# Cross-attention and FP4 feed-forward on one core: batches written out, 128-row context tiles, and jobs placed in a step by the engine that takes them

## The chip, the core and the metric

The kernel runs on one core of a Trainium2 chip. The core has a matrix engine (TensorE, PE in the rows), a vector engine (VectorE, DVE), an activation engine (ScalarE, ACT), GpSimd (POOL) and a queue engine (SyncE, SP) that issues most DMAs. Each engine takes its own instructions in program order and waits for the others by semaphores. The metric is the device time of one execution in microseconds, the median of several; lower is better.

## What is computed

Eight batches. Each has 512 query rows and 1601 context rows of 256 numbers. A layer norm, 16-head cross-attention with a residual, a second layer norm, and a gated feed-forward whose inputs and weights are rounded to a 4-bit grid in blocks of 16:

```python
x = x + xattn(layernorm(x), ctx, ctx)          # heads of 16, softmax over the 1601 keys, biases
def fp4_linear(x, w):                          # blocks of 16 along the last dim
    return einsum('bsk,nk->bsn', fp4_quant_dequant(x), fp4_quant_dequant(w))
h = silu(fp4_linear(y, w_gate)) * fp4_linear(y, w_up)      # y = layernorm(x), 256 -> 704
x = x + fp4_linear(h, w_down)                              # 704 -> 256
```

## The kernel before

**Steps.** The heads are taken in four groups of four, the context in 13 tiles, so a batch has 52 steps (`STEPS`). In step n, PE writes the scores of the tile for two heads (`scores(n, 0)`, L612), then those of the other two (`scores(n, 1)`), into the same two PSUM banks `st`; ACT takes each with an exponential into `prob` (L763, `exps`). Then PE makes products of queries and keys again for the row maxima of a later group (`pair_products`, L626, into `mx`), which DVE reduces (L811, or L820 and L822 for single pieces), and then multiplies the exponentials of step n-1 with the values (`weighted`, L641, into `pvb`).

**Jobs.** Everything else is cut into jobs and hung into the steps by the table `SLOTS`. An entry has two lists. A job of the first list, called side 0 here, is done by PE between `scores(n, 0)` and `scores(n, 1)`; ACT takes its result between its two pairs of exponentials, DVE before the reduction of the step. A job of the second list (side 1) is done by PE behind `weighted`, taken by ACT behind its second pair of exponentials and by DVE behind the reduction. The jobs: `ctxT`, `xnT`, `attT`, `xqT`, `hqT` (transposes, copied by ACT), `q` (L528, ACT L704 and L705), `k` (L538, ACT L715 and L716), `v` (L545, ACT L721), `nm` (transpose of the maxima, L549, five DVE operations from L845), `pvT` (L553, DVE L855 and L857), `o`, `gate`, `up` (L575), `down` (L585), and in the first batch `wT` (transposed FP4 weights, L592, ACT L747). In the loop they all write one PSUM bank, `misc`, in turn: a job's first matmul waits until the job before it has been taken out.

**Batches.** Parts of three batches overlap: "early" jobs prepare the next batch, "att" jobs belong to the present one, "late" jobs end the previous one. The program is a prologue `pre`, the batch `first`, a hardware loop (`Fori`) over six batches, the batch `last`, and `tail`, the feed-forward of the last batch. In the prologue, the first 36 pieces of maxima are made. Inside the loop, waits compare with values held in registers.

**Other queues.** `DVE_EXTRA` places layer norm and quantisation on DVE (among them `xlast`, L926, and `hscale`), `POOL_WORK` the splitting of q and k into bf16 parts and the rounding (L1048 and L1050, L1054 to L1062). SP issues the DMAs in a fixed order; k and q go to scratch memory and come back as `kstack` and `qstack`. The context comes in as `cin` by two DMAs, of 124 and of 123 rows per tile; the raw feed-forward weights (`raw_in`) stand in SP's queue between the others.

Of the kernel before, what the change touches and what calls it, by code (L numbers as in the profile page):

```python
# [16 lines left out]
KROWS = [124, 124] + [123] * 11  # L17
# [36 lines left out]
M_LEAD = 18  # L54
BIAS_AT = STEPS - M_LEAD - 1

# [5 lines left out]

SLOTS = {
    0: ([("v", 5, "att")], []),
    1: ([("v", 6, "att")], [("pvT", 3, "late")]),
    2: ([("attT", 0, "late")], [("attT", 1, "late")]),
    3: ([("o", 0, "late")], []),
    4: ([("o", 1, "late")], []),
    5: ([("ctxT", 0, "early")], []),
    6: ([("ctxT", 1, "early")], [("ctxT", 2, "early")]),  # L70
    7: ([("ctxT", 3, "early")], [("ctxT", 4, "early")]),
    8: ([("ctxT", 5, "early")], [("nm", 1, "att")]),
    9: ([("ctxT", 6, "early")], [("xnT", 0, "early")]),
    10: ([("xnT", 1, "early")], []),
    11: ([("q", 0, "early")], [("wT", 0, "once")]),
    12: ([("k", 0, "early")], [("wT", 1, "once")]),
    13: ([("k", 1, "early")], [("wT", 2, "once")]),
    14: ([("k", 2, "early")], [("pvT", 0, "att")]),
    15: ([("k", 3, "early")], [("wT", 3, "once")]),
    17: ([("q", 1, "early")], []),  # L80
    18: ([("xqT", 0, "late")], [("xqT", 1, "late")]),
    19: ([("gate", 0, "late")], []),
    20: ([("gate", 1, "late")], [("wT", 4, "once")]),
    21: ([("k", 4, "early")], [("nm", 2, "att")]),
    22: ([("gate", 2, "late")], [("wT", 5, "once")]),
    23: ([("gate", 3, "late")], []),
    24: ([("k", 5, "early")], [("wT", 6, "once")]),
    25: ([("gate", 4, "late")], [("wT", 7, "once")]),
    26: ([("gate", 5, "late")], []),
    27: ([("k", 6, "early")], [("pvT", 1, "att")]),  # L90
    28: ([("gate", 6, "late")], []),
    29: ([("gate", 7, "late")], []),
    30: ([("k", 7, "early")], [("wT", 8, "once")]),
    31: ([("up", 0, "late")], [("wT", 9, "once")]),
    32: ([("up", 1, "late")], []),
    33: ([("up", 2, "late")], []),
    34: ([("up", 3, "late")], [("nm", 3, "att")]),
    35: ([("up", 4, "late")], [("wT", 10, "once")]),
    36: ([("up", 5, "late")], [("wT", 11, "once")]),
    37: ([("up", 6, "late")], []),  # L100
    38: ([("up", 7, "late")], []),
    39: ([("hqT", 0, "late")], [("hqT", 1, "late")]),
    40: ([("down", 0, "late")], [("pvT", 2, "att")]),
    41: ([("hqT", 2, "late")], []),
    42: ([("v", 0, "early")], [("hqT", 3, "late")]),
    43: ([("down", 1, "late")], []),
    44: ([("v", 1, "early")], [("hqT", 4, "late")]),
    45: ([("hqT", 5, "late")], []),
    46: ([("v", 2, "early")], []),
    47: ([("down", 2, "late")], [("nm", 0, "early")]),  # L110
    48: ([("v", 3, "early")], [("hqT", 6, "late")]),
    49: ([("hqT", 7, "late")], []),
    50: ([("down", 3, "late")], []),
    51: ([("v", 4, "early")], []),
# [3 lines left out]
    1: ([], [("pvT", 3, "late")]), 2: ([("attT", 0, "late")], [("attT", 1, "late")]), 3: ([("o", 0, "late"), ("o", 1, "late")], []),  # L118
# [12 lines left out]
def slots(kind, n):  # L131
    return (TAIL_SLOTS if kind == "tail" else SLOTS).get(n, ([], []))


PER = {}
for _step in SLOTS.values():
# [18 lines left out]
W_SCALE_AT = {1: 0, 4: 1, 14: 2, 17: 3, 25: 4, 29: 5}
W_POWER_AT = {3: 0, 6: 1, 16: 2, 19: 3, 27: 4, 31: 5}
POOL_WORK = {
    1: [("late", "bias", 0)], 11: [("early", "q", 0)], 12: [("early", "k", 0)], 13: [("early", "k", 1)],
    14: [("early", "k", 2), ("late", "xround", 0)], 15: [("early", "k", 3)], 17: [("early", "q", 1)],
# [7 lines left out]
class Iteration:  # L167
# [8 lines left out]
    def count(self, part, per, k):  # L176

        n = (self.ahead + SHIFT[part]) * per + k
        if isinstance(self.i, int):
            return self.i * per + n  # L180
        assert n > 0
        return self.i * per + n


class SharedBanks:
# [931 lines left out]
```

## Time and profile before

| | us |
|---|---|
| median of 3 runs | 2022.91 (2022.39 to 2029.71) |
| the profiled execution | 2027.88 |
| its span, first to last instruction | 2026.0 |
| prologue, to the first exponential | 127.9 |
| batch `first` | 246.4 |
| six loop batches | 1373.6 (225.4 to 230.5 each) |
| batch `last` | 200.9 |
| `tail` | 77.3 |

The stages are measured between the first exponentials (L763) of the batches. A step's length below is the time from the first exponential of one step to that of the next. In the rows of a timeline, the number in brackets is how long the engine had been idle before the instruction, with what ended the idle time.

### The profile page before, as it was taken

Reading aid. Unit: us, or ns where it says so; the run is one execution under the profiler, and the core shown is the slowest. Engines: PE = TensorE matmul, PEld = TensorE weight load, DVE = VectorE, ACT = ScalarE, POOL = GpSimd, SP = SyncE. Lnnn points to the kernel's source line nnn. Section 1 sums busy time; section 2 is a strip of 40 time slices with the busy share of each in tenths; the row PEclk is TensorE's granted clock in tenths of the full one; section 3 lists DMA queues with packets and bytes.
Section 4 is the critical chain, followed back from the end, with each engine's and each line's share of the span. In section 5 each row is a group of like instructions: output and inputs, shape, how many; then the busy total and the mean of one; then the engine's idle time right before and its main releaser. Section 6 shows DMA issues by size and latency. Waiting matters only on the chain. (4 is left out here: it accounts for less than half of the span.)

```text
span 2026.0 us, 30105 instructions
## 1 busy us (share of the span) xinstructions
PE 1754.9 (87%) x9600; PEld 730.4 (36%) x9600; DVE 1348.5 (67%) x1636; ACT 1127.0 (56%) x2239; POOL 541.8 (27%) x415
## 2 busy tenths in 40 slices
PE   3567688989999899899999899899999899989957
PEld 2222222333343334433343334433344334423425
DVE  1557576776857777676857777576867677576524
ACT  1124466666546665566546665566556665556631
POOL 3203550041320414042320514032320514000414
PEclk9677899999999999999999999999999999999988
DMA  2721431143212332134212322134212422020000
GB/s 66 154 65 27 92 72 33 54 92 65 42 39 52 78 58 40 59 74 79 46 35 52 82 58 38 61 73 71 54 32 49 89 58 39 17 33 1 6 16 11
DMA packets 97768, 109.53 MB, mean 54 GB/s; under 512 B 18484, under 2 KB 83004, under 8 KB 97596
## 3 DMA queue, kind: packets, MB, share of 16 engines
q1 hardware_dynamic: 95500, 106.21, 25.4%
q8 instruction: 89, 1.46, 0.3%
q10 hardware_dynamic: 2096, 1.18, 0.2%
q14 instruction: 83, 0.68, 0.1%
HBM read 76.78 MB, written 30.16 MB: 53 GB/s over the span
## 5 line engine op out<-in xcount | busy, mean ns | idle before, releaser
L763 ACT ACTIVATE prob<-st 123x512 f32<-123x512 f32 (+1 forms) x1664 | 906.9, 601 | 469.1 <-PE st L612 466.9
L811 DVE TENSOR_REDUCE cmx<-mx 128x4 f32<-128x2048 f32 x336 | 769.8, 2291 | 317.6 <-PE mx L626 315.9
L612 PE MATMUL st<-qstack,kstack 112*123 112x512 bf16 (+1 forms) x1664 | 554.6, 401 | 56.3 <-ACT prob L763 29.8
L641 PE MATMUL pvb<-prob,vv 123*17 123x512 f32 (+1 forms) x3328 | 446.2, 609 | 0.0
L612 PEld LDWEIGHTS st<-qstack,kstack 112*123 112x123 bf16 (+1 forms) x1664 | 201.4, 136 | 455.9 <-ACT prob L763 234.6
L626 PE MATMUL mx<-kstack,qstack 48*128 48x512 bf16 (+1 forms) x2048 | 256.6, 343 | 59.7 <-DVE cmx L811 38.1
L575 PE MATMUL misc<-wguT,rowsT 128*128 128x352 f32 x460 | 159.7, 469 | 19.1 <-DVE nmf L845 13.7
L820 DVE TENSOR_REDUCE cmx<-mx 128x2 f32<-128x1024 f32 x96 | 114.9, 1220 | 38.3 <-PE mx L626 38.2
L1021 POOL TENSOR_TENSOR cin<-cin 128x400 f32<-128x400 f32 (+1 forms) x60 | 60.8, 1013 | 284.3 <-ACT cin L716 284.2
L626 PEld LDWEIGHTS mx<-kstack,qstack 48*128 48x128 bf16 x2048 | 57.8, 95 | 216.9 <-issue 133.8
L1021 POOL TENSOR_TENSOR qx<-qx,qp 128x512 f32<-128x512 f32 x16 | 18.5, 1158 | 387.0 <-ACT qp L705 387.0
L641 PEld LDWEIGHTS pvb<-prob,vv 123*17 123x17 f32 (+1 forms) x3328 | 55.4, 95 | 159.8 <-issue 156.7
L538 PE MATMUL misc<-ctxT,wk 128*128 128x400 f32 (+1 forms) x236 | 93.2, 517 | 22.5 <-DVE att L857 12.4
L545 PE MATMUL misc<-wv,ctxT 128*123 128x256 f32 (+1 forms) x392 | 104.8, 413 | 7.1 <-DVE nmf L845 7.1
L575 PEld LDWEIGHTS misc<-wguT,rowsT 128*128 128x128 f32 x460 | 84.9, 191 | 65.8 <-DVE nmf L845 19.1
L1058 POOL TENSOR_TENSOR ht<-ht,mt 128x704 f32<-128x704 f32 x32 | 53.7, 1679 | 184.5 <-DVE mt L939 184.5
L585 PE MATMUL misc<-wdT,hqT 128*128 128x256 f32 x348 | 86.6, 390 | 4.7 <-ACT hqT L742 4.7
L1054 POOL TENSOR_TENSOR ht<-ht,rh 128x704 f32<-128x704 f32 x32 | 44.4, 1386 | 166.7 <-DVE rh L932 165.2
L545 PEld LDWEIGHTS misc<-wv,ctxT 128*123 128x123 f32 (+1 forms) x392 | 78.6, 202 | 27.3 <-DVE nmf L845 10.3
L1034 POOL TENSOR_TENSOR x<-x,bob 128x1024 f32<-128x1024 f32 x8 | 18.7, 2343 | 241.6 <-DMA x<-x 241.6
L867 DVE SCALAR_TENSOR_TENSOR ht<-hqT,misc 128x352 f32<-128x352 f32 x57 | 29.7, 521 | 75.8 <-ACT hqT L730 75.8
L585 PEld LDWEIGHTS misc<-wdT,hqT 128*128 128x128 f32 x348 | 62.4, 189 | 28.0 <-issue 10.7
(169 smaller groups left out, 1546.8 us busy)
## 6 DMA issues: line engine op xcount, KB each, us to landing
kstack<-scr_k SPq DMA_DIRECT2D x384, 100.1 KB, 4.4
scr_k<-cin SPq DMA_DIRECT2D x48, 300.0 KB, 4.3
qstack<-scr_q SPq DMA_DIRECT2D x384, 32.0 KB, 1.9
cin<-ctx_in SPq DMA_DIRECT2D x8, 1353.0 KB
scr_q<-qp SPq DMA_DIRECT2D x16, 384.0 KB, 4.2
scr_k<-cin SPq DMA_DIRECT2D x16, 300.8 KB, 4.5
xn<-x SPq DMA_DIRECT2D x8, 512.0 KB, 6.5
x<-x SPq DMA_DIRECT2D x8, 512.0 KB, 3.6
```

The costliest lines, as they stand in the source:

```text
L538: last = mm(o[:, 0:w], wk[:, h, m * 128:(m + 1) * 128], ctxT[:, h, COFF[n]:COFF[n] + w], start=(h == 0), stop=(h == NC2 - 1))
L545: last = mm(o[0:w, (kt % 2) * E:(kt % 2 + 1) * E], ctxT[:, h, KOFF[kt]:KOFF[kt] + w], wv[:, h, :], start=(kt % 2 == 0 and h == 0), stop=(h ...
L575: last = mm(o[:, 0:IH], rowsT[:, h, t * 128:(t + 1) * 128], wguT[:, h, first:first + IH], start=(h == 0), stop=(h == NC2 - 1))
L585: last = mm(o[:, 0:E], hqT[0:FW[f], f, :], wdT[0:FW[f], f, :], start=(f == 0), stop=(f == NF - 1))
L612: mm(st[0:KROWS[kt], h, :], kstack[:, hd, KOFF[kt]:KOFF[kt] + KROWS[kt]], qstack[:, hd, :], start=True, stop=True).then_inc(st_full, 1)
L626: last = mm(mx[:, q % 2, par, at:at + w], qstack[r0:r0 + LEAD, hd, t * 128:(t + 1) * 128], kstack[r0:r0 + LEAD, hd, k0:k0 + w], start=True ...
L641: last = mm(pvb[32 * h:32 * h + D + 1, :], vv[0:w, kt, HG * g + h, :], prob[0:w, n % 2, h, :], start=(kt == 0), stop=(kt == NKT - 1))
L763: activate(prob[0:KROWS[kt], n % 2, 2 * pair + h, :], st[0:KROWS[kt], h, :], ACT.Exp, scale=SCALE).then_inc(exp_done[2 * pair + h], 1)
L811: v.tensor_reduce(cmx[:, g % 2, h0:h0 + 2, at0:at1 + 1:at1 - at0], mx[:, :, :, :].rearrange("p j h n -> p h j n"), op=ALU.max, axis=AX.X). ...
L820: v.tensor_reduce(cmx[:, g % 2, h0:h0 + 2, at:at + 1], products, op=ALU.max, axis=AX.X).then_inc(max_free, 1)
L1021: g_.tensor_tensor(whole, whole, parts[:, 0, :], ALU.subtract).then_inc(step, 1)
L1058: g_.tensor_tensor(y, y, m, ALU.add).then_inc(h_step, 1)
```

## The change

- `Fori` becomes a Python loop: all eight batches are written out, and no wait compares with a register.
- Context tiles have 128 rows, the thirteenth 65 (before: 124, 124 and eleven of 123). The count of tiles, steps and matmuls stays. The context comes in by three DMAs: 128 rows by 2 tiles, 128 rows by 10, 65 rows.
- `SLOTS` is rewritten. Jobs taken by DVE (`nm`, `pvT`, with `gate`, `up`, `o`, `down` as before) are on side 0; jobs taken by ACT (`q`, all eight `k`, all seven `v`, most transposes) move to side 1. Many late jobs stand one step earlier.
- Prologue (`PRE_SLOTS`): x is loaded before the context; four `k` jobs stand before `xnT` and `q`; only the 26 pieces of the first group's maxima are made, and in the first five steps of `first` four pieces a step instead of two. Five `v` jobs stand at steps 34 to 42.
- Weights: `wk`, `wq` and their biases get a semaphore of their own; `wv`, `wo`, `bv`, `bo` are issued later, and the raw feed-forward weights go from SP's queue to ACT's.
- `tail`: the rounding of xa goes from POOL to DVE, and of the four row tiles of h, POOL and DVE round two each (`hround`).

```diff
-KROWS = [124, 124] + [123] * 11
+KROWS = [128] * (T // 128) + [T % 128]
...
-    12: ([("k", 0, "early")], [("wT", 1, "once")]),
...
+    11: ([("wT", 1, "once")], [("k", 1, "early")]),
...
+PRE_SLOTS = {
+    5: ([("ctxT", j, "early") for j in range(7)], []),
+    11: ([("k", j, "early") for j in range(4)], []),
+    14: ([("xnT", j, "early") for j in range(2)], [("q", 0, "early"), ("q", 1, "early")]),
...
-            with eng.Fori(0, B - 2) as i:
+            for i in range(B - 2):
                 body(Iteration("loop", i, 1))
...
-            for q in (first, first + 1):
+            for q in range(first, first + number):
...
-                sp.dma_start(ctx_rows[0:KROWS[2], 2:NKT, :], ctx_in[bi, n0:T, :].rearrange("(t p) n -> p t n", t=NKT - 2)).then_inc(s_ctx[1], 16)
...
+                for piece, (t0, t1) in enumerate(((0, 2), (2, NKT - 1))):
+                    sp.dma_start(ctx_rows[:, t0:t1, :], ctx_in[bi, t0 * 128:t1 * 128, :].rearrange("(t p) n -> p t n", p=128)).then_inc(s_ctx[piece], 16)
+                sp.dma_start(ctx_rows[0:KROWS[-1], NKT - 1, :], ctx_in[bi, n1:T, :]).then_inc(s_ctx[2], 16)
...
+                    elif what == "xround":
+                        dve.wait_ge(xm_ready, c(1, 1))
+                        v.tensor_tensor(xa[:, :], xa[:, :], mt[:, :], ALU.add).then_inc(xr_step, 1)
```

PE, in a loop batch where the first `k` jobs stand. Before:

```order
L641 MATMUL pvb<-prob,vv 17x512 x4
L612 MATMUL st<-qstack,kstack 123x512 x2
L538 MATMUL misc<-ctxT,wk 128x401 x2
L292 REGISTER_ALU
L612 MATMUL st<-qstack,kstack 123x512 x2
L292 REGISTER_ALU
L626 MATMUL mx<-kstack,qstack 128x512 x2
```

After:

```order
L630 MATMUL pvb<-prob,vv 17x512 x4
L524 MATMUL misc<-ctxT,wk 128x401 x2
L601 MATMUL st<-qstack,kstack 128x512 x4
L615 MATMUL mx<-kstack,qstack 128x512 x4
L630 MATMUL pvb<-prob,vv 17x512 x4
L524 MATMUL misc<-ctxT,wk 128x400 x2
```

The `k` job has moved from between the two pairs of scores to behind `weighted`; the four score matmuls now stand together.

PE, in a loop batch at the `nm` job of the third group. Before:

```order
L641 MATMUL pvb<-prob,vv 17x512 x4
L490 REGISTER_ALU
L548 REGISTER_ALU
L549 MATMUL misc<-ident,nmx 16x128
L612 MATMUL st<-qstack,kstack 123x512 x2
L575 MATMUL misc<-wguT,rowsT 128x352 x2
```

After:

```order
L601 MATMUL st<-qstack,kstack 128x512 x2
L536 MATMUL misc<-ident,nmx 16x128
L601 MATMUL st<-qstack,kstack 128x512 x2
L615 MATMUL mx<-kstack,qstack 128x512 x4
L630 MATMUL pvb<-prob,vv 17x512 x4
L524 MATMUL misc<-ctxT,wk 128x401 x2
L601 MATMUL st<-qstack,kstack 128x512 x2
L562 MATMUL misc<-wguT,rowsT 128x352 x2
```

The `nm` job has moved between the pairs of scores, and a `k` job stands between it and the next `gate` job.

SP, at the start of the prologue. Before:

```order
L351 DMA cin<-ctx_in 124x2x256
L352 DMA cin<-ctx_in 123x11x256
L345 DMA xn<-x 128x4x256
L372 DMA scr_q<-qp 128x1536
```

After:

```order
L357 DMA xn<-x 128x4x256
L364 DMA cin<-ctx_in 128x2x256
L364 DMA cin<-ctx_in 128x10x256
L365 DMA cin<-ctx_in 65x256
L376 DMA scr_q<-qp 128x1536
```

x now comes first, and the long context transfer has 128 rows.

## Rows read from the trace of the kernel before

**Rows 1.** A batch: start:end, length, PE, PEld, DVE, ACT, POOL busy, clock, DMA.

```profile
604.40:834.50 230.10, 212.28 (x1196) 89.26 (x1195) 163.50 (x196) 139.55 (x279) 61.83 (x49) 0.99 0.28 58
```

**Rows 2.** Timeline of a loop step without a job: start, length, engine, line, tiles.

```profile
675.21 2.20 ACT L763 ACTIVATE prob<-st 123x512 f32<-123x512 f32 x4 [0.18 <-PE st L612]
678.23 0.65 PE L612 MATMUL st<-qstack,kstack 112*123 112x512 bf16 x2
678.69 0.60 ACT L763 ACTIVATE prob<-st 123x512 f32<-123x512 f32 x1 [1.28 <-PE st L612]
```

**Rows 3.** Timelines of PE and of ACT at k jobs on side 0.

```profile
656.48 1.51 PE L538 MATMUL misc<-ctxT,wk 128*128 128x401 f32 x4
658.03 0.59 ACT L715 ACTIVATE cin<-misc,bqk 128x401 f32<-128x401 f32 x1 [0.75 <-PE misc L538]
659.00 1.08 ACT L763 ACTIVATE prob<-st 123x512 f32<-123x512 f32 x2
660.34 1.09 ACT L763 ACTIVATE prob<-st 124x512 f32<-124x512 f32 x2 [0.26 <-PE st L612]
664.41 1.09 ACT L763 ACTIVATE prob<-st 124x512 f32<-124x512 f32 x2
```

**Rows 4.** The same at a q job and at a v job on side 0.

```profile
651.92 1.88 PE L528 MATMUL misc<-xnT,wq 128*128 128x512 f32 x4
653.92 0.69 ACT L704 ACTIVATE qx<-misc,bqk 128x512 f32<-128x512 f32 x1 [0.93 <-PE misc L528]
655.07 2.20 ACT L763 ACTIVATE prob<-st 123x512 f32<-123x512 f32 x4
...
801.49 1.89 PE L545 MATMUL misc<-wv,ctxT 128*123 128x256 f32 x8
803.41 0.65 ACT L721 COPY vv<-misc 123x256 f32<-123x256 f32 x2 [0.86 <-PE misc L545]
```

**Rows 5.** A weight transpose on side 1, in the batch `first`.

```profile
199.75 0.52 PE L592 MATMUL misc<-ident,ht 88*128 88x88 f32 x4
200.31 0.45 ACT L747 COPY wguT<-misc 128x352 f32<-128x352 f32 x1 [0.17 <-PE misc L592]
200.66 1.09 ACT L763 ACTIVATE prob<-st 123x512 f32<-123x512 f32 x2
```

**Rows 6.** PE across an edge of the hardware loop.

```profile
834.01 0.64 PE L612 MATMUL st<-qstack,kstack 112*124 112x512 bf16 x2 [3.79 <-issue]
834.48 3.32 PE L545 MATMUL misc<-wv,ctxT 128*123 128x256 f32 x8
```

**Rows 7.** Waits of PE in the six loop batches: total us, times, longest.

```profile
PE misc L575 <- DVE nmf L845: 12.7, 12, 1.2
...
PE misc L575 <- DVE att L857: 2.3, 6, 0.4
```

**Rows 8.** Waits of the whole span in which a DMA was waited for.

```profile
DVE ah L957 <- DMA ht<-w_up: 13.8, 2, 11.5
...
DVE ah L957 <- DMA ht<-w_gate: 13.4, 1, 13.4
```

**Rows 9.** The prologue: a window with the DMA share, then timelines.

```profile
13.00:24.00 11.00, 0.00 (x0) 0.00 (x0) 0.00 (x0) 0.00 (x0) 3.33 (x3) 1.00 0.20 67
...
32.52 1.90 PE L517 MATMUL st<-ident,cin 123*128 123x123 f32 x8 [22.56 <-DMA cin<-ctx_in]
...
51.11 0.36 SPq L372 DMA_DIRECT2D scr_q<-qp  x1
...
76.89 1.03 PE L626 MATMUL mx<-kstack,qstack 48*128 48x512 bf16 x4 [5.72 <-DMA kstack<-scr_k]
...
127.86 1.08 ACT L763 ACTIVATE prob<-st 124x512 f32<-124x512 f32 x2 [0.94 <-PE st L612]
```

**Rows 10.** The tail, POOL: two starts of its quantising, one row tile apart.

```profile
1995.78 1.39 POOL L1054 TENSOR_TENSOR ht<-ht,rh 128x704 f32<-128x704 f32 x1
...
2003.21 1.39 POOL L1054 TENSOR_TENSOR ht<-ht,rh 128x704 f32<-128x704 f32 x1
```

More of the change, by code:

```diff
@@ L84 @@
[L84 to L105, printed above, removed]
@@ L106 @@
-    43: ([("down", 1, "late")], []),
[L107 to L114, printed above, removed]
+    4: ([("o", 1, "late")], [("ctxT", 0, "early")]),
+    5: ([("ctxT", 1, "early")], [("ctxT", 2, "early")]),
+    6: ([("ctxT", 3, "early")], [("ctxT", 4, "early")]),
@@ new lines @@
+    7: ([("ctxT", 5, "early")], [("ctxT", 6, "early")]),
+    8: ([("nm", 1, "att")], [("xnT", 0, "early")]),
+    9: ([("xnT", 1, "early")], [("q", 0, "early")]),
+    10: ([("wT", 0, "once")], [("k", 0, "early")]),
+    11: ([("wT", 1, "once")], [("k", 1, "early")]),
+    12: ([("wT", 2, "once")], [("k", 2, "early")]),
+    13: ([("wT", 3, "once")], [("k", 3, "early")]),
+    14: ([("pvT", 0, "att")], []),
+    15: ([], [("q", 1, "early")]),
+    17: ([("xqT", 0, "late")], [("xqT", 1, "late")]),
@@ new lines @@
+    18: ([("gate", 0, "late")], []),
+    19: ([("gate", 1, "late"), ("wT", 4, "once")], []),
+    20: ([("gate", 2, "late"), ("wT", 5, "once")], []),
+    21: ([("nm", 2, "att")], [("k", 4, "early")]),
+    22: ([("gate", 3, "late")], []),
+    23: ([("gate", 4, "late"), ("wT", 6, "once")], []),
+    24: ([("wT", 7, "once")], [("k", 5, "early")]),
+    25: ([("gate", 5, "late")], []),
+    26: ([("gate", 6, "late")], []),
+    27: ([("pvT", 1, "att")], [("k", 6, "early")]),
+    28: ([("gate", 7, "late")], []),
@@ new lines @@
+    40: ([("pvT", 2, "att")], [("hqT", 2, "late")]),
+    41: ([("hqT", 3, "late")], []),
+    42: ([], [("v", 0, "early")]),
+    43: ([("down", 1, "late")], []),
+    44: ([], [("v", 1, "early")]),
+    45: ([("hqT", 4, "late")], [("hqT", 5, "late")]),
+    46: ([("down", 2, "late")], []),
+    47: ([("nm", 0, "early")], [("v", 2, "early")]),
+    48: ([("hqT", 6, "late")], [("hqT", 7, "late")]),
+    49: ([("down", 3, "late")], []),
+    50: ([], [("v", 3, "early")]),
+    51: ([], [("v", 4, "early")]),
+}
@@ L176, in count @@
     def count(self, part, per, k):
[L178 to L182, printed above, removed]
+        return self.batch(part) * per + k
 class SharedBanks:
@@ L374, in keys_out @@
             def keys_out(it, m):
-                if it.kind == "loop":
-                    sp.lower_val(it.count("early", 4, 1))
                 for g in (2 * m, 2 * m + 1):
@@ L653, in body @@
                         scores(n, 1)
-                    for job in maxima(it, n):
+                    products = maxima(it, n)
+                    for job in products[:2]:
                         pair_products(job)
@@ L659, in body @@
                         weighted(STEPS - 1, "late")
+                    for job in products[2:]:
+                        pair_products(job)
                     for job in jobs(it, n, 1):
@@ L996, in body @@
                             extra(part, what, k)
-                assert all(made[p] == LINKS[p] for p in ("early", "late") if p in it.parts), made
+                assert it.kind == "tail" or all(made[p] == LINKS[p] for p in ("early", "late") if p in it.parts), made
             iterations(dve, body)
```

215 lines of the change are left out of this document (115 added, 100 removed).

## The prediction

> **What bounds the kernel now.** I read the batches first, then one bare step, then the waits. A loop batch takes 230.1 us, and PE is busy in 212.28 of them at a clock of 0.99, full speed; DVE has 163.5, ACT 139.6, POOL 61.8 [rows 1]. So the loop is PE's, with some 18 us of holes, and two questions decide: which holes go, and which are made. In a bare step the exponentials start at 675.21 and the next step's at 678.69, 3.48 us later, while the next scores start at 678.23, 3.02 us after the first exponential [rows 2]. These 3.02 us are a chain of PE and ACT: both exponentials of the first pair, the scores of the second pair, maxima products, `weighted`. ACT is idle for 1.28 us at its end [rows 2]. So PE has a short hole between its two pairs of scores, where it waits for the first exponentials, and none behind `weighted`. A job on side 0 falls into this hole; a job on side 1 lengthens the chain by all of its own time, and its ACT part comes ahead of the next exponential.
>
> **Side 1 for the jobs of ACT.** The length of a step with such a job is 3.02, plus the time from the job's first matmul to ACT's first operation on it, plus ACT's part until the next exponential. A job that stands on side 1 now tests this: weight transpose 199.75, ACT's copy 200.31, exponential 200.66, which is 0.56 + 0.35 behind the point where `weighted` leaves PE [rows 5]; the next exponential indeed starts with the end of the copy, not with its scores.
> - k: 658.03 - 656.48 = 1.55 and 659.00 - 658.03 = 0.97, so 3.02 + 1.55 + 0.97 = 5.54. On side 0 a k step takes 664.41 - 660.34 = 4.07 [rows 3]; with the other k steps I take 4.0. Eight jobs: +12.3 us per batch.
> - q: 2.00 and 1.15 [rows 4], so 6.17, against some 4.3 on side 0 (a matmul pair longer than k's by 0.37 us, rows 3 and 4). Two jobs: +3.8.
> - v: 1.92 and some 0.55 of its two copies [rows 4], so 5.5, against 4.3 on side 0. Six jobs and a half one: +7.8.
> - Transposes on side 1: three more than now, but fewer next to a v job: +1.
> Against it: a side 0 job that follows such a step is covered, since PE writes the next scores early and runs the job while ACT is still at the k result. Four gate or up jobs behind k, and three down jobs behind v, gain 0.2 to 0.3 each: -1.5.
>
> **Side 0 for the jobs of DVE.** `nm` and `pvT` on side 1 are taken only behind the reduction, and the next job, also for `misc`, waits for that. Seven rows of PE's waits name DVE's first operation on `nm` or the last on `pvT`; they go from 12.7 to 2.3 and sum to 44 us in six batches, 7.4 per batch [rows 7]. The steps are longer by somewhat more, 8.3. On side 0 they wait for no reduction of their own step; `nm` may wait a little for the one before (0.2 us each): -8.3 + 0.8. The own PE time of these eight jobs falls into the hole: -2.
>
> **The loop's edge.** At an edge PE is idle for 3.79 us with nothing that it waits for, and the v job behind it takes 3.32 us instead of the 1.89 of its like [rows 6, 4]: 5.2 us per edge, five edges. Written out they go: -5.2 each, which I count per batch. The Trainium skill, Runtime: NRT & Kernel Launch, section Instruction fetch mechanics, says that instructions are fetched ahead in sequence only and that a taken branch to a page not held breaks this; the idle time at the edge agrees, and nothing in the straight-line batches speaks against it. Without the registers a wait with two semaphores costs ACT some 0.06 us more in a bare step (3.54 in the straight-line batches against 3.48 in the loop, an estimate from step lengths): +0.6.
>
> Sum of a loop batch: 12.3 + 3.8 + 7.8 + 1 - 1.5 - 8.3 + 0.8 - 2 - 5.2 + 0.6 = +9.3 us. Six batches: **+56**. Batch `last` has few of the moved jobs (one and a half v) and loses some of the stalls: 0.
>
> **Prologue, now 127.9 us.** Context rows are waited for until 32.5, and from 13 to 24 us the DMA engines are 0.20 busy at 67 GB/s, as if three of sixteen ran [rows 9]. The Trainium skill, DMA: Bandwidth & Descriptors, section Why a DMA increments its semaphore by 16 and not by 1, says that a transfer is cut over the largest number up to 16 that divides its slowest dimension: 3 for 123 rows, 16 for 128. The row agrees with the 3. The sum goes by the row: 67 GB/s at a share of 0.20 are 335 GB/s at a full one, so x, context and two weights (2.7 MB) need 8 us at best and 16 at half the share; with 2 us to start I take 13 for the landing. From there: transposes and four k pieces (ACT first issues six weight DMAs, some 4 us), then xnT, q and POOL's split, which end 23 us later, at some 36. From the end of this split to the first maxima product the queue SP needs what it needs now, 76.89 - 51.11 = 25.8 [rows 9]: 62. The rest, 127.86 - 76.89 = 51.0 now, loses ten of 36 pieces (1.15 us each) and one v job, but the way of the maxima through DVE and SP (5.5 us), now hidden behind those ten pieces, is exposed: 45. First exponential at 106 to 107: **-21.5** (-12 to -30).
>
> **Batch `first`, now 246.4.** Raw weights are waited for by DVE for 13.4 and 11.5 us [rows 8], because SP's queue holds them behind the slow context; both go with the earlier issue, and with them some 9 us of a late context: about -34. The ten pieces come back: in five steps two reductions of 2.3 us and their products stand in a row, some 3 us each more than now, +12. The moved jobs cost what they do in the loop, without the late ones: +16. Sum **-6** (-22 to +8).
>
> **Tail, now 77.3.** The quantising of a row tile of h follows at 7.43 us (2003.21 - 1995.78) [rows 10], four in series between DVE and POOL. With two engines DVE becomes the one that sets the end; I take one round as saved, **-8** with the rounding of xa (-12 to -2).
>
> Total: -21.5 - 6 + 56 + 0 - 8 = +20.5 on the profiled execution's 2027.9. That execution lies 5 us above the median, 2022.9, and the loop's edges, the part that varies, are gone afterwards, so I do not carry the 5 us in full: **2044 us**, 1.0% above the median.
>
> **Rivals.**
> 1. Faster: the moved ACT jobs cost half of what the chain says, since the following step makes the time up (PE has written its scores by then, and any side 0 job is covered). The 24 us per batch become 12, in seven batches -84: **1960**, or 1975 with a smaller gain elsewhere. For it: the covered jobs above. Against it: the four k steps stand in a row with nothing on side 0 between them, and in a row nothing can be made up. The point from which it decides: at a cost of 1.2 instead of 1.4 us per moved job the kernel comes out level.
> 2. No difference (2013 to 2033): the same mechanisms, with the two sums closer, 7 us per batch instead of 9.3.
> 3. Slower than forecast, **2075**: DVE becomes a bound as well. In `first` it holds ten more pieces and the weights' scales, and `hscale` (2.4 us) meets a reduction (2.29) and an `up` in steps of 3.7: 2 us per batch more, and a colder PE clock in the holes.
> 4. The prologue gains nothing, because the weights and the queue of small transfers set it, not the context: +15, 2059.
>
> **How the numbers follow.** About 0.5% is what a measurement of this kernel can tell from no change: 2012.8 to 2033. The forecast has 0.5, the first rival 0.17, the second 0.18, the third 0.1, the fourth 0.05. With a spread of some 20 us around the forecast that makes faster 0.2, same 0.22, slower 0.58. The range, 2000 to 2072, leaves out most of the first rival and the far end of the third.
>
> **What would show it.** Right: a k job's row on PE behind `weighted`, ACT idle up to it, the next exponential at its end, steps of 5.5 us four times in a row; PE's waits on DVE's `nm` and `pvT` operations gone; no PE idle time of 3.8 us between batches; loop batches of 238 us that are all alike; first exponential near 106; a context transfer at a DMA share far above 0.2. Wrong: loop batches at 225 or less, which is the first rival; PE waiting at L615 for DVE's reduction, the third; first exponential behind 115, the fourth.

## The result, and the profile after

The changed kernel takes **2104.98 us** (median of 4 runs, 2101.66 to 2106.55) against 2023.93 us for the kernel before on the same chip: a ratio of 1.0393, 95% interval 1.0367 to 1.0418. It is slower, as forecast, but by four times as much (+81 us, not +20), and it lies above the range. Its profiled execution took 2106.43 us, with a span of 2104.6.

The stages of the two spans, cut at the first exponential of each batch (the tail begins at the end of the last exponential), beside the forecast's own terms:

| stage (us) | before | forecast | after | missed by |
|---|---|---|---|---|
| prologue, to the first exponential | 127.9 | 106.4 | 103.0 | -3.4 |
| batch `first` | 246.4 | 240.4 | 254.5 | +14.1 |
| six loop batches | 1373.6 | 1429.4 | 1473.2 | +43.8 |
| batch `last` | 200.9 | 200.9 | 197.5 | -3.4 |
| tail | 77.3 | 69.3 | 76.4 | +7.1 |

So the miss lies in the loop batches, in `first` and in the tail. The same cut of a loop batch as in [rows 1] reads, for the kernel after (start:end, length, PE, PEld, DVE, ACT, POOL busy, granted clock, DMA share, GB/s; two short stretches of the batch below it):

```profile
847.60:1093.30 245.70, 218.15 (x1194) 80.86 (x1194) 160.56 (x196) 139.53 (x278) 60.53 (x49) 0.98 0.26 54
893.00:901.00 8.00, 5.90 (x20) 1.73 (x20) 3.87 (x7) 3.91 (x8) 3.56 (x4) 0.79 1.00 165
926.00:938.00 12.00, 9.08 (x41) 2.44 (x40) 5.71 (x3) 6.18 (x12) 3.35 (x3) 0.72 0.74 108
```

The batch is 15.6 us longer, and PE has 27.6 us of holes instead of 17.8. It is also busier by 5.9 us with the same matmuls. A part of this is the clock: there are stretches with a granted clock of 0.79 and 0.72, and in them the same instructions take longer.

The forecast's first mechanism stands in the timeline of PE around two k jobs on side 1, each with a `gate` job on side 0 behind it (start, length, engine, line, tiles, idle before and what ended it):

```profile
979.11 1.61 PE L524 MATMUL misc<-ctxT,wk 128*128 128x400 f32 x4
980.56 0.59 PE L601 MATMUL st<-qstack,kstack 112*128 112x512 bf16 x2
981.89 1.45 PE L562 MATMUL misc<-wguT,rowsT 128*128 128x352 f32 x4 [0.74 <-ACT cin L722]
...
992.38 1.61 PE L524 MATMUL misc<-ctxT,wk 128*128 128x400 f32 x4
993.83 0.60 PE L601 MATMUL st<-qstack,kstack 112*128 112x512 bf16 x2
995.16 1.45 PE L562 MATMUL misc<-wguT,rowsT 128*128 128x352 f32 x4 [0.74 <-ACT cin L722]
```

and in that of ACT:

```profile
989.39 2.16 ACT L769 ACTIVATE prob<-st 128x512 f32<-128x512 f32 x4 [1.03 <-PE st L601]
994.03 0.60 ACT L721 ACTIVATE cin<-misc,bqk 128x400 f32<-128x400 f32 x1 [2.47 <-PE misc L524]
994.52 0.59 ACT L722 ACTIVATE cin<-misc,bqk 128x400 bf16<-128x400 f32 x1
995.00 1.08 ACT L769 ACTIVATE prob<-st 128x512 f32<-128x512 f32 x2
```

From 989.39 to 995.00 is 5.61 us; the forecast had 5.54, and q and v steps read 6.16 and 5.55 against 6.17 and 5.5. What was not forecast is the last row of PE's timeline: the `gate` job, which was to be covered by ACT's work on k, waits for the end of that work, since both use the one bank `misc`. In the waits of PE in this batch (total us, times, longest), it has a row of its own, and `nm` on side 0 has one too:

```profile
PE st L601 <- ACT prob L769: 11.6, 13, 1.4
...
PE misc L536 <- DVE nmx L839: 3.5, 4, 1.6
...
PE misc L562 <- ACT cin L722: 3.0, 4, 0.7
...
PE misc L465 <- DVE xa L953: 1.4, 1, 1.4
```

The prologue did what was said. Its windows, then the first context transposes and the end of the q split (answering to the first, second and third of [rows 9]):

```profile
1.00:8.00 7.00, 0.67 (x4) 0.70 (x4) 2.49 (x11) 1.28 (x1) 6.71 (x2) 1.00 0.75 237
8.00:12.00 4.00, 0.50 (x3) 0.10 (x3) 3.97 (x2) 0.59 (x1) 4.00 (x1) 1.00 0.92 257
...
11.92 1.97 PE L501 MATMUL st<-ident,cin 128*128 128x128 f32 x8 [3.50 <-DMA cin<-ctx_in]
...
33.44 0.38 SPq L376 DMA_DIRECT2D scr_q<-qp  x1
```

### The profile page after: what moved, and what is told of

Read it like the earlier page. It is cut to its first block and busy times, and to the rows that moved or that the text cites. A ratio compares the mean times of both kernels' runs of the same rounds, so it can differ in the third digit from the quotient of the medians.

```text
span 2104.6 us, 26231 instructions
## 1 busy us (share of the span) xinstructions
PE 1788.9 (85%) x9600; PEld 668.2 (32%) x9600; DVE 1351.2 (64%) x1641; ACT 1127.7 (54%) x2239; POOL 518.9 (25%) x405
## 5 line engine op out<-in xcount | busy, mean ns | idle before, releaser
L769 ACT ACTIVATE prob<-st 128x512 f32<-128x512 f32 (+1 forms) x1664 | 905.2, 600 | 369.9 <-PE st L601 368.9
L601 PE MATMUL st<-qstack,kstack 112*128 112x512 bf16 (+1 forms) x1664 | 551.8, 391 | 125.5 <-ACT prob L769 99.2
L630 PE MATMUL pvb<-prob,vv 128*17 128x512 f32 (+1 forms) x3328 | 448.7, 612 | 0.0
L601 PEld LDWEIGHTS st<-qstack,kstack 112*128 112x128 bf16 (+1 forms) x1664 | 145.7, 99 | 537.4 <-ACT prob L769 325.8
L615 PE MATMUL mx<-kstack,qstack 48*128 48x512 bf16 (+1 forms) x2048 | 257.0, 344 | 36.1 <-DVE cmx L824 21.6
L562 PE MATMUL misc<-wguT,rowsT 128*128 128x352 f32 x460 | 160.7, 472 | 24.3 <-ACT cin L722 17.8
L615 PEld LDWEIGHTS mx<-kstack,qstack 48*128 48x128 bf16 x2048 | 56.6, 95 | 184.3 <-issue 116.7
L833 DVE TENSOR_REDUCE cmx<-mx 128x2 f32<-128x1024 f32 x86 | 103.2, 1219 | 16.6 <-PE mx L615 16.6
L721 ACT ACTIVATE cin<-misc,bqk 128x400 f32<-128x400 f32 (+1 forms) x59 | 35.2, 596 | 140.5 <-PE misc L524 126.6
L727 ACT COPY vv<-misc 128x256 f32<-128x256 f32 (+1 forms) x96 | 31.4, 375 | 142.9 <-PE misc L532 142.9
L630 PEld LDWEIGHTS pvb<-prob,vv 128*17 128x17 f32 (+1 forms) x3328 | 55.5, 95 | 162.6 <-issue 151.1
L532 PE MATMUL misc<-wv,ctxT 128*128 128x256 f32 (+1 forms) x384 | 104.6, 417 | 0.0
L532 PEld LDWEIGHTS misc<-wv,ctxT 128*128 128x128 f32 (+1 forms) x384 | 72.0, 198 | 53.1 <-issue 43.2
```

What stands on the lines that cost most here:

```text
L532: last = mm(o[0:w, (kt % 2) * E:(kt % 2 + 1) * E], ctxT[:, h, KOFF[kt]:KOFF[kt] + w], wv[:, h, :], start=(kt % 2 == 0 and h == 0), stop=(h ...
L562: last = mm(o[:, 0:IH], rowsT[:, h, t * 128:(t + 1) * 128], wguT[:, h, first:first + IH], start=(h == 0), stop=(h == NC2 - 1))
L601: mm(st[0:KROWS[kt], h, :], kstack[:, hd, KOFF[kt]:KOFF[kt] + KROWS[kt]], qstack[:, hd, :], start=True, stop=True).then_inc(st_full, 1)
L615: last = mm(mx[:, q % 2, par, at:at + w], qstack[r0:r0 + LEAD, hd, t * 128:(t + 1) * 128], kstack[r0:r0 + LEAD, hd, k0:k0 + w], start=True ...
L630: last = mm(pvb[32 * h:32 * h + D + 1, :], vv[0:w, kt, HG * g + h, :], prob[0:w, n % 2, h, :], start=(kt == 0), stop=(kt == NKT - 1))
L769: activate(prob[0:KROWS[kt], n % 2, 2 * pair + h, :], st[0:KROWS[kt], h, :], ACT.Exp, scale=SCALE).then_inc(exp_done[2 * pair + h], 1)
```

## Experiments

Twelve kernels. A figure for a stage comes from each one's profiled execution, cut as above. One of them (e4_tail_rounds) was executed once, so its time has no interval.

**The loop's edge alone** (e1_written_out). The kernel before with its hardware loop written out, nothing moved.

```diff
-            with eng.Fori(0, B - 2) as i:
+            for i in range(B - 2):
```

> The kernel before with only the hardware loop written out; tables, tiles, prologue and tail stay. If the idle 3.8 us and the slow v job at each of the five edges come from the loop's branch: -5.2 us per edge, 26 in all, 1997 us, and loop batches of some 224 us, all alike. If they come from something else at a batch's start (the maxima of the next group, the residual), or if the longer straight code costs fetches of its own: within 5 us of the kernel before.

Measured: 2000.3 us, ratio 0.9882 (0.9861 to 0.9903). The six loop batches fall from 1373.6 to 1349.6 us. So the edge costs about what was read from [rows 6] (1997 us and batches of 224 were expected), and writing the loop out is a gain of 1.2% by itself. The slow v job behind the edge is the clock's doing: from 834.4 to 837.8 us the kernel before has a granted clock of 0.56, behind 3.79 us in which PE was idle, and in stretches of 4.5 to 5 us at the four other edges it reads 0.50 to 0.66. Bare steps take 3.55 us there, 0.06 more than in the loop, as the sum had it (+0.6 per batch).

**The k jobs alone** (e2_k_side1). The kernel before with its eight k jobs on side 1.

```diff
-    24: ([("k", 5, "early")], [("wT", 6, "once")]),
+    24: ([], [("wT", 6, "once"), ("k", 5, "early")]),
```

> The kernel before, hardware loop and all, with one edit: the eight k jobs (and the two weight transposes beside them) on side 1 instead of side 0. Chain theory: a k step goes from 4.0 to 5.5 us, and a gate or up job behind it waits some 0.7 us for ACT to empty the one bank misc, 0.3 of it in the step's length: +13 us per batch, seven batches, 2115 us. If the next step makes half of it up: +6 per batch, 2065 us.

Measured: 2130.48 us, ratio 1.0528 (1.0508 to 1.0547). The chain theory holds and the rival falls; the cost is 15.2 us per loop batch, above the 12.3 of the sum and the 13 expected here. In three of the eight steps an `nm` or `pvT` stands behind k on side 1; these grow by 2.1 to 2.6 us. Of the five others, four grow by 1.5 to 1.8.

**The moved jobs back** (e3_side0_again). The kernel after with 12 of its 17 jobs for ACT back on side 0 (k0 to k3, k5, k7, q1, v0, v1, v3, v4, v5), `nm` and `pvT` left on side 0.

```diff
-    24: ([("wT", 7, "once")], [("k", 5, "early")]),
+    24: ([("k", 5, "early")], [("wT", 7, "once")]),
```

> The changed kernel with twelve of the seventeen moved jobs back on side 0 (six k, one q, five v: those whose step has nothing else there); the first batch's weight transposes change sides with them. Chain theory: -1.5 for a k, -1.9 for q, -1.25 for a v, and 0.3 where a gate or down job follows: -18 us per batch in seven batches, 1980 us. If the batches grew mainly by the jobs of DVE on side 0 (nm waiting for the maxima) and by DVE's own work: -20 to -40 in all, 2070 us.

Measured: 1970.76 us, ratio 0.974 (0.9721 to 0.9758): 134 us faster than the kernel after, where the chain theory had 125 (1980 us) and its rival 35. The loop batches take 1355.9 us instead of 1473.2, which is 19.6 us per batch or 1.63 us per job, the jobs behind them included. This run holds its own control: k5 and k7 are back on side 0, k4 and k6 are not. PE's waits in a loop batch show the row of the bank halved, from four to two:

```profile
PE misc L562 <- ACT cin L722: 1.5, 2, 0.7
```

The steps behind k5 and k7 take 3.72 us (3.99 in the kernel after), those behind k4 and k6 still 3.99; a `gate` or `up` step behind another one takes 3.68. So a job behind a k job costs 0.3 us, where the forecast had a gain of 0.2 to 0.3.

**The tail's rounding of h** (e4_tail_rounds). The kernel after with all four row tiles of h rounded on POOL, as before; the rounding of xa stays on DVE.

```diff
-TAIL_POOL = {1: POOL_WORK[1], 19: [("late", "hscaled", 0)], 20: [("late", "hround", 0)], 21: [("late", "hscaled", 2)], 22: [("late", "hround", 2)]}
+TAIL_POOL = {1: POOL_WORK[1], 19: [("late", "hscaled", 0)], 20: [("late", "hround", 0), ("late", "hscaled", 1)], 21: [("late", "hround", 1), ("late", "hscaled", 2)],
+             22: [("late", "hround", 2), ("late", "hscaled", 3)], 23: [("late", "hround", 3)]}
```

> The changed kernel with the rounding of h in the tail left to POOL for all four row tiles, as before; the rounding of xa stays on DVE. If DVE became the end's bound by taking two tiles: two tiles follow in 14.9 us again instead of 16.9, the tail goes from 76.4 to some 74 us. If the split was worth something and the tail's lost gain lies elsewhere: 80 us or more.

Measured (one execution): 2101.29 us, tail 74.3 us against 76.4, as expected. With DVE's share the rounding takes 29.0 us from first to last operation, with POOL alone 31.1. Among all kernels with the rounding of xa on DVE, the tails run from 74.3 to 78.6 us with POOL alone (six) and from 75.8 to 76.8 with DVE's share (four). So a gain of 7 us is excluded. Cut at PE's first `down` matmul, the tails sort better: it starts 52.3 to 53.4 us behind the last exponential in the six and 54.6 to 55.5 in the four; what follows takes 22.0 to 22.4 us in five of the six and 21.2 to 21.4 in the four. So DVE's share costs about 1 us, but the sixth, e7_all_side0, takes 25.2 us for this last part, which no run explains.

**The tiles alone** (e5_rows_128). The kernel before with 128-row context tiles and their three loads.

```diff
-KROWS = [124, 124] + [123] * 11
+KROWS = [128] * (T // 128) + [T % 128]
```

> The kernel before with 128-row context tiles alone (their loads with three waits too); loop, order of jobs and prologue's order stay. Theory: in the prologue the context lands at 12 to 14 us instead of 32.5, and the way from the q split to the first product is unchanged, so the first exponential comes some 17 us earlier, near 111. In batch first the waits for late context and raw weights (33.6 us of stretched steps 3 to 6 and 19) shrink by 25 to 30, near 219. Loop, last and tail unchanged within 1 us per batch: about 1978 us, ratio 0.978. Rival: the prologue is set by the six weight transfers and the small bias transfers on ACT's queue, and the gain ends at some 5 us; first unchanged: 2019.

Measured: 1979.42 us, ratio 0.9781 (0.9734 to 0.9829). The first exponential comes at 108.8 us, and `first` falls to 228.5, not to 219: DVE still waits 12.6 us for a piece of the raw weights (`w_up`), and 27.2 for `w_up` and `w_gate` in the kernel before. The six loop batches lose 7.3 us too: a bare step takes 3.42 us instead of 3.48. The longer tiles are worth 42 us (35 to 54), half of what the whole change lost.

**The pieces back in the prologue** (e6_pieces_back). The kernel e3_side0_again with the ten maxima pieces of the second head group where they were before.

```diff
-            if it.kind == "first" and n < M_LATE:
-                first, number = M_GROUP + 4 * n, 4
-            if part not in it.parts or it.kind == "pre" and first >= M_GROUP:
+            if part not in it.parts:
```

> The kernel e3_side0_again with the ten maxima pieces of the second head group back in the prologue. Theory: the prologue grows by about 8 us (ten pieces of 1.15 us less what they cover), to 110; steps 0, 1, 2 and 4 of batch first, which take 7.5, 9.1, 6.9 and 13.0 us in e3, fall to near 4 to 5 where the added products and reductions set them, some -15 us: near 1963 us. Rival: the steps are long for another reason (DVE stretched beside POOL's weight rounding, late weights, POOL's queue); then first stays near 235 and the time rises by 8, to 1979.

Measured: 1961.18 us, ratio 0.9697 (0.9651 to 0.9742). The prologue grows by 6.9 us, `first` falls by 12.5.

**ACT's jobs on side 0** (e7_all_side0). 15 of the 17 (all but k4 and k6), with the rows around them moved by a step to make room.

```diff
-    9: ([("xnT", 1, "early")], [("q", 0, "early")]),
-    10: ([("wT", 0, "once")], [("k", 0, "early")]),
+    10: ([("q", 0, "early")], []),
+    11: ([("k", 0, "early")], [("wT", 0, "once")]),
...
+    15: ([("k", 3, "early")], [("wT", 3, "once")]),
```

> The changed kernel with every job of ACT on side 0 except k4 and k6 (q0, v2 and v6 too), nm and pvT on side 0, the transposes of h two by two from step 39 as before, and the tail's rounding of h on POOL alone. Theory of the chain: against e3 (226 us per loop batch) q0 gives back 1.9, v2 and v6 1.5 each, the transposes of h some 2: a loop batch of 219, six of them 1315; with first near 233, last 195 and a tail of 74 the sum is 102 + 233 + 1315 + 195 + 74 = 1919 us. Rival: with every side 0 filled the one misc bank becomes the chain (each job waits for the one before) and the batch stays at 225: 1955.

Measured: 1987.35 us, ratio 0.9823 (0.9777 to 0.987). Both theories missed (1919 and 1955 us): it is slower than e3_side0_again, which has fewer of them there. POOL's timeline in a loop batch shows why: k3 now comes two steps later, and the rounding of xa is queued behind its split.

```profile
865.22 0.95 POOL L1054 TENSOR_TENSOR cin<-cin 128x400 f32<-128x400 f32 x1 [4.76 <-ACT cin L722]
866.25 0.85 POOL L1056 TENSOR_TENSOR cin<-cin,one 128x400 bf16<-128x400 f32 x1
867.18 0.89 POOL L1058 TENSOR_TENSOR cin<-cin 128x400 bf16<-128x400 f32 x1
868.02 2.35 POOL L1081 TENSOR_TENSOR xa<-xa,mt 128x1024 f32<-128x1024 f32 x1
```

At its end PE stands 4.14 us for the rounded rows, which DVE scales last, and the transposes behind the wait are slow:

```profile
875.13 1.09 PE L467 MATMUL misc<-ident,xa 128*128 128x128 f32 x4 [4.14 <-DVE xa L955]
```

**The jobs of DVE back on side 1** (e8_dve_side1). The kernel e7_all_side0 with `nm` and `pvT` on side 1; k4 and k6 on side 0.

```diff
-    21: ([("nm", 2, "att")], [("k", 4, "early")]),
+    21: ([("k", 4, "early")], [("nm", 2, "att")]),
```

> The kernel e7_all_side0 with the eight jobs of DVE (nm, pvT) back on side 1, as before the change, k4 and k6 now on side 0. Theory, by the terms of the prediction: the stalls on DVE come back, +8.3 - 0.8 + 2 = +9.5 us per batch, and k4 and k6 on side 0 give 3.1: +6.4 per batch, seven batches +45 against e7. Rival: the stalls were worth less than forecast, since another job's wait takes their place (nm waits for its own maximum, 0.9 us each): +2 per batch or less, below +15 in all.

Measured: 2013.3 us, ratio 0.9959 (0.9941 to 0.9976): +26, not +45. The loop batches are longer by 3.0 us each; with k4 and k6 credited at the 1.63 us measured above, the stalls are worth 6.3 us per batch where the sum had 9.5 (an estimate, since this run moves both kinds of job). The part that was too small in it is the wait of `nm` on side 0: step 34 takes 4.33 us with it on side 0 and 3.58 with it on side 1, so 0.75 and not 0.2.

**POOL's order** (e9_rounding_first). The kernel e7_all_side0 with POOL's rounding of xa ahead of the split of k3.

```diff
-    14: [("early", "k", 3), ("late", "xround", 0)],
+    14: [("late", "xround", 0), ("early", "k", 3)],
```

> The kernel e7_all_side0 with one thing changed: on POOL the rounding of xa stands ahead of the split of k3, not behind it. Theory: step 17 of a loop batch (10.8 us in e7, 7.5 or 6.0 in e3) is long because k3 moved to step 15 and POOL's rounding of xa, and with it DVE's last scaling and the transposes xqT, are queued behind its split; so step 17 falls by 3 to 4.8, a loop batch to 225 or 226, the kernel to about 1964 us. Rival: the transposes wait for something else (the bank, the colder clock), and step 17 keeps above 9: 1985.

Measured: 1967.84 us, ratio 0.9729 (0.97 to 0.9759). Step 17 falls from between 9.7 and 10.8 us to between 6.2 and 7.7: the queue was the cause of that wait. It does not bring back the 1919 us. A loop batch takes 226.1 us, against 226.0 in e3_side0_again, which has three jobs fewer on side 0: steps 0 to 9 are shorter by 2.7 us in sum, and steps 37 to 48, where the transposes of h stand two by two, longer by 3.

**DVE's last scaling one step earlier** (e11_last_scale_15). The kernel e6_pieces_back with this alone:

```diff
-    13: [("late", "xpower", 0)], 16: [("late", "xlast", 0)],
+    13: [("late", "xpower", 0)], 15: [("late", "xlast", 0)],
```

> The kernel e6_pieces_back with one thing changed: DVE's last scaling of xa stands in step 15, not 16, so ahead of one more reduction. In e6 the rounding ends at 855.8, the scaling waits behind the reduction of step 16 until 860.4, and the first transpose of xqT idles 2.16 us for it. Theory: the wait goes, 2.2 us per batch in six loop batches: 1961 - 13 = 1948 us. Rival: the scaling pushes the reduction of step 16 back and PE waits there instead: 1961.

Measured: 1942.8 us, ratio 0.961 (0.9574 to 0.9645), so 18 us for one entry of a table. Step 17 takes 4.16 us in every loop batch, where it took 5.97 in five of them and 7.55 in the first. There PE came out of the wait slow: its next scores and products read 1.06 and 1.03 us, where 0.60 and 0.61 are usual (kernel e6_pieces_back):

```profile
409.53 0.67 PE L462 MATMUL misc<-ident,xa 128*128 128x128 f32 x4 [2.16 <-DVE xa L952]
410.00 1.06 PE L598 MATMUL st<-qstack,kstack 112*128 112x512 bf16 x2
410.99 1.03 PE L612 MATMUL mx<-kstack,qstack 48*128 48x512 bf16 x4
```

**The best order of these** (e10_best). The kernel e6_pieces_back with q0 on side 0 too (k0 to k3 and q1 moved a step or two for it), POOL's order and DVE's last scaling as above, h rounded on POOL alone in the tail.

> The kernel e6_pieces_back with q0, k3 and q1 moved so that q0 stands on side 0 too, the rounding of xa ahead of k3 on POOL, DVE's last scaling of xa one step earlier (15), and the tail's rounding of h on POOL alone. Theory: steps 9 to 16 give 1.5 us per batch, the wait of xqT for the last scaling (2.2 us in a loop batch of e6) goes, the tail gives 2: 1961 - 6 x 3.7 - 2 = 1937 us. Rival: the wait only moves to the next job and the gain is the tail's and 1.5 per batch: 1950.

Measured: 1925.89 us, ratio 0.952 (0.9491 to 0.9549). All six loop batches take 220.8 us each. PE's holes have fallen to 12 us, and its busy time with them:

```profile
774.10:994.90 220.80, 208.69 (x1196) 80.53 (x1195) 162.44 (x197) 139.59 (x278) 61.45 (x49) 1.00 0.29 60
```

**Weights later in `first`** (e12_weights_later). The kernel e10_best with DVE's and POOL's work on the first two weight pieces moved behind the layer norm of the next batch.

```diff
-W_SCALE_AT = {1: 0, 4: 1, 14: 2, 17: 3, 23: 4, 28: 5}
-W_POWER_AT = {3: 0, 6: 1, 16: 2, 19: 3, 25: 4, 30: 5}
+W_SCALE_AT = {1: 0, 7: 1, 14: 2, 17: 3, 23: 4, 28: 5}
+W_POWER_AT = {6: 0, 9: 1, 16: 2, 19: 3, 25: 4, 30: 5}
```

> The kernel e10_best with DVE's and POOL's work on the first two pieces of raw weights moved, in batch first alone: the power of piece 0 from step 3 to 6, the scales of piece 1 from 4 to 7, its power from 6 to 9, behind the layer norm's operations of the same step. Theory: steps 5, 6 and 8 of batch first (9.97, 6.20, 8.52 us in e10; 4.24, 4.17, 4.16 in a loop batch) are long because small DVE operations that start beside a POOL operation end only with it (2.1, 2.3, 1.9, 2.8, 1.5 us instead of 0.2 to 0.7), so steps 5 and 6 fall by 5 to 8 in sum, step 8 stays, batch first from 223.4 to some 217, and the kernel to 1920 us. Rival: the steps are long by the amount of DVE's own work, which only moves: first stays within 2 us.

Measured: **1919.9 us**, ratio 0.9491 (0.9465 to 0.9516), 5.1% below the kernel before and 8.8% below the one after. `first` falls by 7.2 us; steps 5 and 6 go from 9.97 and 6.20 us to 4.17 each, step 1 from 6.48 to 4.59, step 8, which was to stay, from 8.52 to 7.07, and step 9 rises from 3.48 to 6.79, where the rounding now stands.

## Why the prediction was right or wrong

**The direction was right, by its own mechanism.** The sum said that jobs of ACT on side 1 lengthen the chain by all of their time and that this outweighs the rest. With 12 of them back the kernel is 2.6% faster than the kernel before. The first rival (half the cost, 1960 us) is excluded by the steps of 5.60 us four in a row. The single steps came within 0.07 us.

**The step that failed first: "a side 0 job that follows such a step is covered"** (-1.5 us per batch). PE writes the next scores early, as said, but the job behind them needs `misc`, and ACT holds it until it has read k twice. The row of 0.74 us, four times per batch, and its halving with k5 and k7 back on side 0 show it. The kernel has one such bank, which the forecast named for `nm` and `pvT` and forgot for k; what a second bank would do no run shows. Twelve jobs were priced at 17.1 us less 0.7 for those covered, 16.4, and measured 19.6. Step by step, the 19.6 are 10.1 for six k jobs (9.2 in the sum), 7.4 for five v jobs (6.0), 1.5 for q (1.9), 0.9 for the three jobs behind them (-0.7), and -0.3 elsewhere. So the covered jobs are half of the excess of 3.2. Another 1.3 lie in steps 10 and 0, which take 7.1 to 7.3 us instead of 5.6 in two and in three of the six batches, of which more below. By the same ratio all 17 cost 28.0 us where the sum had 23.4, an estimate.

**Stalls of DVE's jobs**, forecast at -9.5 per batch with the wait of `nm` and PE's own time, estimated from e8_dve_side1 as -6.3. The seven rows of [rows 7] did go. In their place came 3.5 us of waits for `nm`'s own maximum, where 0.8 was forecast: on side 0 it comes before the reduction that it needs has ended.

**The edge**: forecast -5.2 per batch and +0.6 for dearer waits, measured -4.0 with these waits in it (24 us in six). The sum counted five edges as six, and it went by the longest: PE's idle times at the five sum to 16.7 us. The tiles, for whose effect on a loop batch the sum had no term, give -1.2. Together: +28.0 - 6.3 - 4.0 - 1.2 = 16.5 us per batch, against 16.6 measured and 9.3 forecast. Two of these four are estimates, so the agreement to 0.1 is luck; but the two mis-sized terms (4.6 and 3.2) are most of the miss.

**`first`**: the ten pieces were right (+12 forecast, 12.5 measured). Two steps failed. One is +16 for the moved jobs: it is the 12.3 of k and the 3.8 of q, without the 7.8 of v, though no v job is a late one. Twelve of the 17 measure 16.6; the other five are worth some 7 more, an estimate from `first` in e7_all_side0, e8_dve_side1 and e10_best. The other is "both go with the earlier issue ..., about -34". The 128-row tiles alone bring 17.9 of it, and what is left for all that the sum did not price otherwise, by the stage lengths, is 246.4 + 12.5 + 16.6 + 7 - 254.5 = 28. The waits for the DMA went; what was hidden behind them did not, and PE now waits 18.8 us for DVE's reductions in `first`. DVE's timeline of the kernel after in step 4 of `first`:

```profile
136.90 2.12 DVE L912 TENSOR_SCALAR ve<-mv 128x4 f32<-128x4 f32 x1
139.06 0.17 DVE L913 TENSOR_SCALAR hv<-ve 128x4 f32<-128x4 f32 x1
139.13 2.31 DVE L914 TENSOR_SCALAR rs<-ve 128x4 int32<-128x4 int32 x1
141.54 2.29 DVE L824 TENSOR_REDUCE cmx<-mx 128x4 f32<-128x2048 f32 x1
```

and POOL's beside it:

```profile
136.65 2.34 POOL L1105 TENSOR_TENSOR ht<-ht,mt 88x1024 f32<-88x1024 f32 x1 [11.40 <-DVE mt L998]
139.07 2.35 POOL L1107 TENSOR_TENSOR ht<-ht,mt 88x1024 f32<-88x1024 f32 x1
141.50 1.93 POOL L1109 TENSOR_TENSOR ht<-ht,sh 88x1024 f32<-88x1024 f32 x1
```

Operations on four elements per row take 2.1 and 2.3 us and end with POOL's (at 139.02 and 138.99, and at 141.44 and 141.42). The reduction behind them starts late, and PE waits for it. With the weights moved the same operations read 0.17 and 0.16 (kernel with the weights later):

```profile
126.41 0.17 DVE L911 TENSOR_SCALAR ve<-mv 128x4 f32<-128x4 f32 x1
126.62 0.17 DVE L912 TENSOR_SCALAR hv<-ve 128x4 f32<-128x4 f32 x1
126.69 0.16 DVE L913 TENSOR_SCALAR rs<-ve 128x4 int32<-128x4 int32 x1
```

**The prologue** was right in its mechanism: context at 11.9 us (13 forecast), q split ended at 33.4 (36), first exponential at 103.0 (106 to 107). But the tiles alone reach 108.8, and so does the new order of the prologue with the pieces put back: the reordering gave nothing that the tiles had not. The pieces gave 6.9 us here and cost 12.5 a stage later, which the forecast's own terms, 6 and 12, had already said.

**The tail**: -8 forecast, -0.9 measured. The rounding of xa on DVE gave its 2.3 us (it ends 23.7 us behind the last exponential, before 26.0). The failed step is "one round as saved", and with it the path: the rounding lost 2.1 us of the 7.4, and the end of the tail did not follow it. POOL's timeline shows two of its tiles 16.9 us apart, where two rounds took 14.9 before [rows 10], and POOL idle for 7.35 us of it:

```profile
2064.44 1.39 POOL L1085 TENSOR_TENSOR ht<-ht,rh 128x704 f32<-128x704 f32 x1 [34.87 <-DVE rh L959]
...
2081.33 1.39 POOL L1085 TENSOR_TENSOR ht<-ht,rh 128x704 f32<-128x704 f32 x1 [7.35 <-DVE rh L959]
```

It waits for the scales of its next tile, which DVE works out only behind its own six rounding operations. DVE "sets the end" of the rounding, as the forecast wrote, and no round of it was priced. Its six operations also stand ahead of the gate products of the next tiles, for which PE waits, so that PE's first `down` comes 55.05 us behind the last exponential, as in the kernel before (55.09) and not as in e4_tail_rounds (52.3). From there PE and ACT take the tiles one after the other:

```profile
2078.19 1.45 PE L562 MATMUL st<-wguT,rowsT 128*128 128x352 f32 x4 [3.20 <-DVE ht L880]
...
2087.87 0.87 PE L570 MATMUL mx<-ident,ht 128*128 128x128 f32 x6
...
2092.56 0.87 PE L570 MATMUL st<-ident,ht 128*128 128x128 f32 x6
2094.30 3.02 PE L574 MATMUL mx<-wdT,hqT 128*128 128x256 f32 x12 [0.87 <-ACT hqT L748]
2097.25 0.88 PE L570 MATMUL mx<-ident,ht 128*128 128x128 f32 x6
```

A row tile follows at 4.69 us. Measured from the last exponential, the rounding of the kernel after ends earlier than that of e4_tail_rounds (65.2 us and 66.6), and PE's last transposes end later (69.9 and 67.8): two tiles that are ready together do not help an engine that takes them in turn and begins late. So the earlier xa is worth 1.5 to 3.0 us in five of the six tails with h on POOL alone (74.3 to 75.8 against 77.3), and DVE's share gives part of it back.

**The third rival** was half right: PE's clock did fall, and in `first` the sign that the forecast named for it, PE at L615 waiting for DVE's reduction, is there (18.8 us in nine waits). In the six loop batches these waits sum to 1.9 us, so there DVE did not become the bound. The top of the range, 2072, rested on it, and was too low because no bound was set on the moved jobs from above: each was priced from one row, and its follower at a gain.

**The clock is a small part.** The six loop batches have a mean granted clock of 0.98 in the kernel after and 0.99 in the one before and in e3_side0_again. By the clock records PE is busy at the lower level for 48.3, 29.8 and 23.5 us of them. If work takes twice as long there (an estimate; the scores shown above go from 0.60 to 1.06 us), that is 24, 15 and 12 us of lost time. So the clock accounts for some 9 of the 99.6 us between the kernels before and after. What else makes PE's busy time longer, 218.15 against 210.81 us in a batch of the kernel with the jobs back, is open.

## What to carry to other kernels

When a job is moved between two places of an in-order queue, price three things from rows: its own chain, the job behind it (who still holds the bank or buffer that it needs), and every other queue whose order the move changes; the second and third were the misses here, and the third made an experiment slower in turn. Where two engines hand work back and forth, a job belongs into the hole of the engine that computes it, not to the engine that takes it. And undo a large change part by part: of this one, which lost 4%, the longer tiles, the written-out loop and the side of DVE's jobs are gains. With most of ACT's jobs back on side 0, the ten pieces back in the prologue, and DVE's last scaling, POOL's rounding and the first weight pieces moved by some steps, they make 5%.

## What the runs showed of the hardware

**DVE beside POOL.** In the rows above, and in others of their kind (a step of a reciprocal square root on 128x4 at 1.92 us, a cast of 16x128 at 1.60), a DVE operation on SBUF starts beside a POOL operation and ends with it. Not every one does. The scales of a tile in the tail of the kernel after, DVE and then POOL:

```profile
2068.18 0.88 DVE L956 TENSOR_REDUCE ah<-ht 128x44 f32<-128x704 f32 x1
2069.09 0.97 DVE L957 TENSOR_SCALAR sh<-ah 128x44 f32<-128x44 f32 x1
2070.09 0.43 DVE L958 RECIPROCAL rh<-sh 128x44 f32<-128x44 f32 x1
2070.55 1.25 DVE L959 TENSOR_SCALAR rh<-rh 128x44 f32<-128x44 f32 x1
...
2068.34 1.67 POOL L1090 TENSOR_TENSOR ht<-ht,mt 128x704 f32<-128x704 f32 x1 [2.51 <-DVE mt L968]
2070.09 1.67 POOL L1092 TENSOR_TENSOR ht<-ht,mt 128x704 f32<-128x704 f32 x1
```

The two operations with a scalar take 0.19 us each alone; here they end with POOL's. The reciprocal between them takes 0.43 and the reduction of 128x704 from SBUF 0.88 with POOL or without, and reductions that read PSUM keep 2.29 us throughout. Held up were operations with a scalar, a cast, and operations with two tiles in SBUF. I had taken an operation's own duration as its price, whatever ran beside it. The Trainium skill, SBUF — State Buffer, section SBUF: two separate sides, says that the two engines share one port pair, held by one of them for a whole instruction while the other blocks, and that on DVE's side this concerns operations in a two-port mode or with two inputs in SBUF. The traces agree as far as they go: they do not show an operation's mode. The moved weights gave back 7.2 us of one batch.

**PE's clock after a wait.** A k job's four matmuls take 1.61 us in most places of the kernel after and 2.38 in step 10, behind a hole of 1.41 us and other short ones. From 897.2 to 899.6 the granted clock is 0.67, so part of it at the lower level of 1.2 GHz:

```profile
894.02 0.88 PE L601 MATMUL st<-qstack,kstack 112*128 112x512 bf16 x2 [1.41 <-ACT prob L769]
897.21 2.38 PE L524 MATMUL misc<-ctxT,wk 128*128 128x401 f32 x4
...
897.20:899.60 2.40, 2.40 (x9) 1.27 (x6) 1.96 (x5) 0.00 (x0) 0.00 (x0) 0.67 1.02 148
```

Step 10 then takes 7.23 us instead of 5.61. It does so in two loop batches of six, with the same work; in three others it is step 0 that takes 7.1 to 7.3 us instead of 5.57. The kernel e6_pieces_back has the same hole of 2.16 us ahead of the transposes of xqT in all its seven last batches. Behind it step 17 takes 7.55 us in two of them and 5.97 in five. The scores behind the hole at 409.53, shown under e11_last_scale_15, read 1.06 us at a granted clock of 0.64 (409 to 412.5), and in a later batch 0.60 at 1.00 (861 to 865.5):

```profile
861.77 0.63 PE L462 MATMUL misc<-ident,xa 128*128 128x128 f32 x4 [2.16 <-DVE xa L952]
862.23 0.60 PE L598 MATMUL st<-qstack,kstack 112*128 112x512 bf16 x2
```

So the same hole costs 1.6 us more in some batches than in others. Taken away in e11_last_scale_15, it gave 3.4 us in step 17 of two batches and 1.8 in each of the five others. The six loop batches gained 15.4 us in all, of which 2.9 lie in steps 34 to 37, which the edit does not touch; no run explains these.
